# Graph network layer: row numbers past the end for edges outside a step's block, and gathers that leave such rows out

## What is computed

```python
z = h @ W_func.T
concat_z = jnp.concatenate([z[edge_src], z[edge_dst], w], axis=-1)
e = jax.nn.leaky_relu(concat_z @ W_att.T, negative_slope=NEG_SLOPE)[:, 0]
m = jax.ops.segment_max(e, edge_dst, num_segments=N)
e_exp = jnp.exp(e - m[edge_dst])
denom = jax.ops.segment_sum(e_exp, edge_dst, num_segments=N)
alpha = e_exp / denom[edge_dst]
agg = jax.ops.segment_sum(alpha[:, None] * z[edge_src], edge_dst, num_segments=N)
```

## Time and profile before

| | |
|---|---|
| median of 3 runs | 2501.78 us (2500.49 to 2505.84) |
| the profiled execution | 2505.82 us |
| its span in the trace | 2504.1 us |
| PE, PEld busy | 1926.2, 1530.7 us |
| DVE, ACT busy | 1556.8, 611.9 us |
| POOL busy | 1668.5 us |
| granted PE clock, mean | 0.859 |
| moved by DMA | 378.65 MB, 151 GB/s |

### The profile page before, as it was taken

How to read it: one execution, slowest core, us unless ns; L and a number is a source line. 1 busy time by engine, 2 the same in 40 slices (tenths; PEclk the granted TensorE clock), 3 DMA queues, 4 the chain that set the end, 5 groups by cost and what they waited for, 6 DMA issues and landing times.

```text
span 2504.1 us, 39252 instructions
## 1 busy us (share of the span) xinstructions
PE 1926.2 (77%) x11133; PEld 1530.7 (61%) x11133; DVE 1556.8 (62%) x3687; ACT 611.9 (24%) x2634; POOL 1668.5 (67%) x1278
## 2 busy tenths in 40 slices
PE   3899577659887777777878767878775778999992
PEld 1444476547766665665666656656654667888882
DVE  4778599877766565566566655656654883226263
ACT  1333388611111111111111111111101323433430
POOL 5554466688888888888888888888884277316164
PEclk8999756569988898898888888888887888999996
DMA  5766788534454444445544444455456455437363
GB/s 155 205 205 189 253 299 294 190 98 133 124 151 127 123 128 123 123 124 134 140 127 123 127 123 123 123 146 132 123 125 182 133 163 153 129 111 199 102 191 96
DMA packets 310586, 378.65 MB, mean 151 GB/s; under 512 B 119740, under 2 KB 263832, under 8 KB 307376
## 3 DMA queue, kind: packets, MB, share of 16 engines
q1 hardware_dynamic: 168932, 234.02, 30.1%
q0 software_dynamic: 141568, 143.66, 23.3%
HBM read 291.57 MB, written 84.76 MB: 150 GB/s over the span
## 4 chain that ended last, share of the span: by engine, by line
PE 34%; POOL 19%; DVE 9%; issue 8%; DMA 5%; ACT 2%; DVEq 2%; SPq 0%; ACTq 0%; POOLq 0%
PE bank L692 32%; POOL wexp L633 17%; DMA wexp<-xn_rows,a_src 4%; PE bank L1018 1%; POOL g_all L679 1%; DVEq L1508 1%; DVE work L1744 1%; DVE work L1749 1%; DVE st L1752 1%; DVE onehot L1668 1%; DVE acc L1680 1%; DVE acc L1766 1%; DVE work L1518 0%; DVE work L1526 0%; SPq L339 0%
## 5 line engine op out<-in xcount | busy, mean ns | idle before, releaser
L633 POOL DMA_INDIRECT wexp<-xn_rows,a_src x900 | 1126.8, 1252 | 274.0 <-issue 258.4
L692 PE MATMUL bank<-wexp,onehot 125*125 125x257 f32 x1800 | 548.7, 459 | 269.9 <-DMA wexp<-xn_rows,a_src 158.8
L692 PEld LDWEIGHTS bank<-wexp,onehot 125*125 125x125 f32 x1800 | 393.5, 228 | 404.2 <-issue 295.1
L1680 DVE TENSOR_TENSOR acc<-bank,acc 125x257 f32 x450 | 190.8, 424 | 419.9 <-PE bank L692 385.0
L1668 DVE TENSOR_SCALAR onehot<-iota_r,a_rel,a_hi 125x125 f32<-125x125 f32 x900 | 289.1, 389 | 0.0
L679 POOL DMA_INDIRECT g_all<-y_d,work x100 | 126.4, 1264 | 218.9 <-DMA y_d<-g_all 117.6
L692 PE MATMUL bank<-g_all 128*128 128x256 f32 x1040 | 238.0, 382 | 8.0 <-DVE g_all L1908 4.6
L692 PEld LDWEIGHTS bank<-g_all 128*128 128x128 f32 x1040 | 193.6, 191 | 33.8 <-issue 6.1
L692 PE MATMUL bank<-work,w_s 128*128 128x250 f32 x800 | 189.0, 378 | 27.9 <-ACT work L1155 27.1
L692 PE MATMUL bank<-s_p,wexp 128*128 128x49 bf16 (+1 forms) x3600 | 143.7, 203 | 62.4 <-DVE wexp L1473 60.6
L692 PEld LDWEIGHTS bank<-work,w_s 128*128 128x128 f32 x800 | 150.4, 191 | 55.7 <-ACT work L1155 35.3
(11 more groups left out here) (269 smaller groups left out, 2739.1 us busy)
## 6 DMA issues: line engine op xcount, KB each, us to landing
wexp<-lr_d SPq DMA_DIRECT2D x75, 750.0 KB
wexp<-in_attr SPq DMA_DIRECT2D x25, 896.0 KB
g_all<-sorted_d SPq DMA_DIRECT2D x65, 256.0 KB
y_d<-g_all SPq DMA_DIRECT2D x65, 256.0 KB, 3.0
wexp<-xn_rows,a_src POOLq DMA_INDIRECT x900, 3.9
sorted_d<-spare SPq DMA_DIRECT2D x48, 256.0 KB, 5.5
sorted_d<-spare SPq DMA_DIRECT2D x24, 384.0 KB, 4.6
work<-xn_rows SPq DMA_DIRECT2D x38, 224.0 KB
```

What stands on the lines that cost most here:

```text
L633: pool.indirect_dma_start(ring[:, 2 * z + k, 0:D], None, xn_rows, bass.IndirectOffsetOnAxis(ap=a_src[:, n // CS, j:j + 1], axis=0)).then_i ...
L692: return pe.matmul(o, l, r, start=first, stop=last_, **kw)
L1680: v.tensor_tensor(to, bank[3 + z % 2][0:R, 0:D + 1], to, ALU.add).then_inc(s("summed"), 1)
```

## The change

The row numbers in `a_src` are raised by 65536 for every edge outside its step's block. On VectorE, `index_rows` makes a mark for edges inside the block from `rel_l` (one comparison and a fused comparison and product), subtracts 65536 times it from the source, and `index_columns` adds 65536 again with its copy out of PSUM; for the other two tables it adds 0. The order of the three tables becomes relative destination, source, high part, and the semaphore counts of `l_done` follow. The gathers of the step loop get a greatest row number, 6249, and are told that a row past it is no error: it is not gathered, and the ring keeps what it held. GpSimd clears the ring's parts that nothing has written before, three pieces of `wexp`, at the start.

```diff
+NO_ROW = 65536.0
@@ gpsimd, start
             pool.memset(eps_c[:], EPS).then_inc(s("consts"), 1)
+            for k in range(HS, 2 * HS):
+                pool.memset(wexp[:, k * LPAD + LROW:(k + 1) * LPAD if k < 2 * HS - 1 else 2 * ZS * (D + 1)],
+                            0.0).then_inc(s("gaps"), 1)
@@ gpsimd, step_rows
                     pool.indirect_dma_start(ring[:, 2 * z + k, 0:D], None, xn_rows,
-                                            bass.IndirectOffsetOnAxis(ap=a_src[:, n // CS, j:j + 1], axis=0)
-                                            ).then_inc(s(f"rows_in{z // 3}"), 16)
-
+                                            bass.IndirectOffsetOnAxis(ap=a_src[:, n // CS, j:j + 1], axis=0),
+                                            bounds_check=N - 1, oob_is_err=False).then_inc(s(f"rows_in{z // 3}"), 16)
+
+            pool.wait_ge(s("gaps"), HS)
             for n in range(ZS - 2):
                 step_rows(n)
@@ tensor, index_columns
-                    last = pe.transpose(bank[INDEX_BANKS[a]][0:R, j * QS:(j + 1) * QS], (src_f, rel_l, hi_l)[a // 2][:, k * R:(k + 1) * R],
+                    last = pe.transpose(bank[INDEX_BANKS[a]][0:R, j * QS:(j + 1) * QS], (rel_l, junk[0:QS], hi_l)[a // 2][:, k * R:(k + 1) * R],
                                         ident[0:QS, 0:QS])
@@ vector, index_rows
-                v.tensor_copy(src_f, src_i).then_inc(s("l_done"), 1)
+                t.did(v.tensor_copy(src_f, src_i))
                 t.did(v.tensor_copy(dst_f, dst_i))
...
-                v.wait_ge(s("l_done"), 2)
+                v.wait_ge(s("l_done"), 1)
                 t.settle()
+                t.did(v.tensor_scalar(junk[0:QS], rel_l, 0.0, None, ALU.is_ge))
+                t.settle()
+                t.did(v.scalar_tensor_tensor(junk[0:QS], rel_l, float(R), junk[0:QS], ALU.is_lt, ALU.mult))
+                t.settle()
+                v.scalar_tensor_tensor(junk[0:QS], junk[0:QS], -NO_ROW, src_f, ALU.mult, ALU.add).then_inc(s("l_done"), 1)
@@ vector, index_columns
-                to = (a_src, a_rel, a_hi)[a // 2]
+                to = (a_rel, a_src, a_hi)[a // 2]
                 j0 = CS * (a % 2)
-                v.tensor_copy(to[:, :, j0:j0 + CS].rearrange("p q j -> p j q"),
-                              bank[INDEX_BANKS[a]][0:R, 0:CS * QS].rearrange("p (j q) -> p j q", q=QS)).then_inc(s("a_done"), 1)
+                v.tensor_scalar(to[:, :, j0:j0 + CS].rearrange("p q j -> p j q"),
+                              bank[INDEX_BANKS[a]][0:R, 0:CS * QS].rearrange("p (j q) -> p j q", q=QS),
+                                NO_ROW if to is a_src else 0.0, None, ALU.add).then_inc(s("a_done"), 1)
```

## The result

The change made the kernel slower: 2559.35 us, the median of 4 runs (2546.79 to 2567.26), against 2501.14 us (2493.37 to 2505.84), a ratio of 1.023 [1.018, 1.028]. The forecast of 2439 us had the wrong sign, and its range ended at 2545. The profiled execution took 2546.79 us, the shortest of the four.

A forecast was written before the change was run, and what follows sets the result against it. GpSimd's issue of gathers was taken as the bound: 2505.8 - 67.3 (dropped rows) + 4.4 (prologue) = 2442.9 us profiled, or 2439 us against the median, ratio 0.975. The range was 2420 to 2545 us.

The forecast's parts named there:

- So 56% of the kernel is the GpSimd queue issuing gathers with no room in it.: Step loop: GpSimd's 900 gathers, with their gaps, fill about 1408 us and bound the kernel.
- If a dropped row costs nothing, 12,500 x 5.38 ns = 67.3 us go.: Gathers: leaving out 12,500 rows gives GpSimd back 67.3 us, with bounds of 0 and 125 us.
- rival B: Gathers: a dropped row costs as much as a kept one, 2506 us; chance 0.20; sign: minimum still 1207 ns.
- The slope itself: GpSimd's cost per gathered row, 5.38 ns, from 942 ns for 75 rows (line 614) and 1211 for 125 (line 633).
- I take nothing, nearest to the 23 ns: Gathers: comparing row numbers with the bound is priced at 0, with bounds of 0 and 605 us.
- the near row: Scatters of 125 rows last 1188 ns, gathers 1211; 23 ns for each of 900 gathers suggests 20.7 us for comparing.
- rival A: Every gather: comparison costs more than dropped rows give back, 2591 us; chance 0.20; sign: median gather moves up.
- break-even of 70 ns a gather: Comparison cost at which the net relief of 62.9 us is used up; also 0.56 ns a row.
- Prologue, 4.4 us.: VectorE before the first gather: three new index operations add 4.4 us, with bounds of 0 and 8.7 us.
- Line 1387's additions and the memsets at nothing: Prologue: six copies turned into additions, and three GpSimd memsets covered by an 18.1 us wait, cost nothing.
- It passes through whole: Step loop: the 67.3 us relief shortens the kernel fully, since TensorE's slack is 178 us over the stretch.
- Rival C: Step loop: TensorE takes over, half the relief lost to slot waits, clock perhaps lower; 2472 us; chance 0.05.

The follow-up runs named there:

- the bound alone: Kernel before with only the greatest row number added to the gathers, nothing marked or dropped: 2562.65 us, 1.0239.
- its repetition: The changed kernel run once more, beside the other experiments, against the kernel before: 2561.54 us, 1.0241.
- the marks alone: Changed kernel without the bound and with offset 65536 set to 0, keeping VectorE's index work and the memsets, against the kernel before: 2501.51 us, 1.0002.
- every row dropped: Changed kernel with all 112,500 row numbers of the step loop raised past the end, against the kernel before: 2563.99 us, 1.0249.
- 115 rows: Kernel before with gathers of 115 rows instead of 125, the other rows left out, the ring cleared once: 2486.46 us, 0.9944.
- one small memset a step: Gathers of 128 rows, plus a 128x4 GpSimd memset each step between slot wait and gathers, against the kernel before: 2309.13 us, 0.9236.

## Why the prediction was wrong

**"So 56% of the kernel is the GpSimd queue issuing gathers with no room in it."** Right, and every sum of the loop rests on it: 50.2 us more of gathers gave 50.3 us more of loop; for the bound alone it was 57.6 and 58.1.

**"If a dropped row costs nothing, 12,500 x 5.38 ns = 67.3 us go."** This is the step that failed. A dropped row is prepared like a kept one, so the term is 0, its lower bound and rival B's mechanism. The gather with nothing in it (1267 ns) beside the one with everything (1267 ns) shows it. I had taken "fewer rows in the instruction" for "rows skipped in the instruction": the 75 rows of line 614 are a smaller index list, while a dropped row keeps its place in the list and its packet (141,568, as before).

**The slope itself** was wrong too. The two durations are right, and on line 633 itself 75 rows take 946 ns; but they are not two points of one line, as 85 and 100 rows show. Among 85, 115 and 125 rows a row costs 2.7 ns, so by my estimate even rows that cost nothing would have given 12,500 x 2.7 = 34 us. I had noted that the two rows differ in their tensors; what matters is the number of rows, and not in proportion.

**"I take nothing, nearest to the 23 ns"**, for the comparison. It costs 56 ns in the median gather and 56 to 64 in the mean, so 50 to 58 us in all: inside the bounds of 0 and 605, and above the 20.7 us of the near row. This is the second term that failed: I put it at nothing, against my own near row. Its form was wrong as well: I scaled rival A in nanoseconds a row looked at, but 75 rows pay 61 ns and 125 rows 56. Rival A had the right sign and place; its break-even of 70 ns a gather was not even reached, so with the forecast relief the kernel would still have been a little faster. The loss is A's price with B's zero to set against it. I held them apart as rivals with 0.20 each, and never worked out both together.

**The rule of rival B**, in which the Trainium skill ("DMA: Bandwidth & Descriptors", the anatomy of one DMA on the SWDGE path) calls descriptor generation "small, variable", pointed the right way for dropped rows: its result was that they give nothing back, and the trace agrees, since 112,500 of them gave nothing. But that doesn't come from a small cost of preparing rows: a gather costs GpSimd from 946 to 1211 ns by its number of rows, and 900 of them bound the loop. A dropped row gives nothing back because it is prepared like any other.

**Prologue, 4.4 us.** Up to TensorE's next block it is borne out, with 4.3 us, but partly by luck: VectorE spent 8.6 us, and the subtractions gave 4.3 back. In the kernel's time it isn't seen: with these operations and without the bound it stands at 1.0002 [0.9985, 1.0019]. The first gather started between 477.1 and 483.3 us over the change, its repetition, the marks alone and every row dropped, and between 479.5 and 484.8 us in the four kernels of 125 rows without the marks. So whether the 4.3 us reach the loop isn't shown. I had also misread the subtractions of before: two of the six were slow, not one. The first, from 82.8 us, took 4.66 us beside the multiplication of 82.84 us, and the last, from 88.5 us, took 4.62 us beside that of 88.43 us. Now one of the six is slow, and the other collision fell on line 1383.

**Line 1387's additions and the memsets at nothing:** right. The additions last 960 ns at the median, where the copies took 958 to 960:

```profile
L1397 DVE TENSOR_SCALAR a_rel<-bank x2: 958/960/961, 117.6 to 127.1; 125x450 f32<-125x450 f32 x2
L1397 DVE TENSOR_SCALAR a_src<-bank x2: 956/960/965, 136.5 to 145.9; 125x450 int32<-125x450 f32 x2
```

**"It passes through whole", against TensorE's slack of 178 us.** Not tested by the change, which gave no relief. The experiments bear out the size, 178 us, but not that it comes by itself. With 115 rows 23.4 us passed whole; with one small memset a step 1406.4 - 1217.8 = 188.6 us passed. With much cheaper gathers alone (75, 100 and 128 rows) TensorE's waits for landing rows went away, and other waits made the loop longer than before. Rival C put a cost on waits for a slot, and on a lower clock; the granted clock in fact rose in the denser stretch, from 0.88 to 0.94.

**What the profile was to show:** the sign named for A came, since the median moved up. The sign for B came in substance: the minimum is 1261 ns and not 1207, but it rose with the median, and there is no spread downwards. The mean is 1308 ns and not 1177. Packets did not fall by 12,500 but by none. The gaps stayed at 0.30 us, as said.

## What to carry to other kernels

Where the issue of indirect DMAs is the bound, count what an option adds to every DMA first. Skipping rows saved bytes here and none of the issuing engine's time, so a bound that is to save work would have to make whole DMAs disappear, or be applied where transfers are the limit; neither was tried. Try other numbers of rows: 128 rather than 125 makes each gather 265 ns cheaper, which is worth more here than any skipping, though only with a paced producer (alone it made the kernel slower, 1.0378). And when the producer gets cheaper, look whether it now runs into the end of its ring: a paced producer beat an eager one by 284 us, so try a few beats.

## What was not expected of the hardware

- A bound on an indirect DMA adds 56 to 61 ns to its issue on GpSimd, with 75 rows or 125, none dropped or all; where a row past it is an error, 71 ns.
- A dropped row keeps its packet and moves 4 bytes. With every row dropped the DMA engines' share from 600 to 1880 us fell from 0.49 to 0.20, and the loop was no shorter than with none dropped.
- A gather of 128 rows costs GpSimd 946 ns, one of 125 rows 1211 ns.
- Gathers that run into the ring's end slow the loop below TensorE's ability: 3.29 us a step, where 2.71 are possible. VectorE, ScalarE and GpSimd then have waits that the profile labels "remote" (GpSimd 102.8 us, 47 times), which no loop without this condition has. Why the engines then go slower stays open.
